# One attention stage of a sandwich block, its per-tile loop rewritten as seven steps that interleave two tiles

## The chip, the cores and the metric

The kernel runs on the 8 NeuronCores of one Trainium2 chip. Every core runs the same program on its own 2048 of the 16384 tokens, and the cores exchange nothing. The metric is the device time of the slowest core, in microseconds (us).

## The reference

```python
def attn(x, W_qkv, b_qkv, W_out, b_out):          # D_MODEL 1024, 16 heads of 64
    qkv = (x @ W_qkv + b_qkv).reshape(B, S, 16, 3 * 64)
    q, k, v = qkv[..., :64], qkv[..., 64:128], qkv[..., 128:]
    scores = einsum('bshd,bsgd->bshg', q, k) / 8   # over the heads of one token
    context = einsum('bshg,bsgd->bshd', softmax(scores), v)
    return context.reshape(B, S, 1024) @ W_out + b_out

def ffn(h, Wg, Wu, Wd):                            # 8 experts, FFN 4096, all summed
    for wg, wu, wd in zip(Wg, Wu, Wd):
        acc += (silu(h @ wg) * (h @ wu)) @ wd

x = x + layernorm(attn(layernorm(x)))
x = x + layernorm(ffn(layernorm(x)))
```

The attention is over the 16 heads of a single token, so no token looks at another. The scores are 16 x 16 for each token, and they are worked out on VectorE, with a token on each partition.

## The kernel before

The program has three stages. Stage A (lines 190 to 356) does the attention for 16 tiles of 128 tokens each, one tile after the other. Stage B (lines 402 to 489) is the FFN: for 64 groups of 512 hidden features (8 experts x 8 groups), and in each for 4 blocks of 512 tokens, TensorE makes 4 x 8 matmuls with Wg (L437), as many with Wu (L442) and 8 x 4 with Wd (L468). ScalarE applies silu, VectorE multiplies and adds into `acc` in SBUF. Stage C (lines 519 to 575) transposes `acc` back, normalises it, adds the residual and stores.

The buffers of stage B lie where those of stage A lay. So the first weight load of stage B (L409) waits for the last transpose, the last transposed copy and the last statistic of stage A.

Each engine runs its instructions in the order in which the Python code appends them to that engine's list (`steps`). The helper `op(engine, function, channel)` appends an instruction that raises a semaphore, and `channel.wt(engine, token)` appends a wait for it. A wait therefore stands in one engine's list and holds all that is behind it there.

For one tile, stage A before the change does, in this order:

1. Line 201: `ln_stats` on the residual `xf`: a sum (VectorE L141), a square (ScalarE L143), a second sum (VectorE L145), small VectorE operations, Ln and Exp (ScalarE L153, L155), and L157. Then L205 writes the normalised tile `ln1` in bf16.
2. Lines 208 to 213: eight TensorE transposes of `ln1` (L181) and one VectorE copy to `ln1T` (L184).
3. Lines 216 to 233: the QKV projection. Six output pieces of 512 columns, each a bias matmul (L223) and 8 matmuls (L227) into one of two PSUM buffers `ps_mm`. ScalarE evacuates each piece to `qkv` (L232).
4. Lines 236 to 307: the attention itself, almost all of it on VectorE: `vtc` (L237), four products of q and k (L248) that are folded by additions (L252) and a sum (L257), the softmax with one Exp on ScalarE (L270), four products with v (L290), and their foldings (L294, L302) into `ctxt`.
5. Lines 309 to 325: eight transposes of `ctxt`, the copy to `ctxT` (L184), and the output projection, two pieces of a bias matmul (L319) and 8 matmuls (L322) into `ps_att`.
6. Lines 327 to 337: `ln_stats` on `ps_att`, the normalisation to `tmpl` (L332) and the residual addition into `xf` (L336).
7. Lines 339 to 355: `ln_stats` on the new `xf`, `ln2tok` (L343), eight transposes, and the copy to `ln2T` (L184). After every fourth tile SyncE spills `xf` to HBM (L352) and reloads it for the tiles two blocks later.

The second set of statistics shares this helper, so L141, L143 and L145 each occur three times in a tile. `qkv` has one buffer. The evacuation of tile t into it waits for the end of tile t-1's attention (line 218).

Of the kernel before, what the change touches and what calls it, by code (L numbers as in the profile page):

```python
# [8 lines left out]
BF16 = mybir.dt.bfloat16  # L9
# [17 lines left out]
def build(mode='full', nt_lim=NT):  # L27
# [161 lines left out]
    ph = probsn  # L189
    for t_i in range(nt_lim):  # L190
        j, i = divmod(t_i, 4)
        jp = j % 2
        p2 = t_i % 2
        xt = xf[:, jp, i]

        if t_i == 0:
# [6 lines left out]
        if t_i >= 2:  # L203
            TB.wt('v', tok_ln1_tr[t_i - 2])
        w_ln1 = op('v', lambda v, xt=xt, p2=p2: v.tensor_scalar(  # L205
            ln1[:, p2], xt, stats[:, p2, 4:5], stats[:, p2, 5:6], ALU.mult, ALU.add), VE)

        VE.wt('t', w_ln1)
        if t_i == 0:
# [3 lines left out]
        trt, ev1 = transpose_batch(lambda k, p2=p2: ln1[:, p2, k * 128:(k + 1) * 128], ln1T[:, p2])  # L213
        tok_ln1_tr[t_i] = trt

        VE.wt('t', ev1)
        if t_i >= 1:
            VV.wt('s', tok_hm_done[t_i - 1])
        for n in range(6):
            b = n % 2  # L220
            if n_qg[0] - 2 in tok_qkv_evac:
                QE.wt('t', tok_qkv_evac[n_qg[0] - 2])
            op('t', lambda t, n=n, b=b: t.matmul(ps_mm[:, b], ones1[:],  # L223
                                                 bq_sb[:, n * 512:(n + 1) * 512], start=True, stop=False))
            mt = None
            for k in range(8):
                mt = op('t', lambda t, n=n, b=b, k=k, p2=p2: t.matmul(  # L227
                    ps_mm[:, b], ln1T[:, p2, k], wqkv_sb[:, k, n * 512:(n + 1) * 512],
                    start=False, stop=(k == 7)), MM if k == 7 else None)
            MM.wt('s', mt)  # L230
            tok_qkv_evac[n_qg[0]] = op(
                's', lambda s, n=n, b=b: s.activation(qkv[:, n * 512:(n + 1) * 512], ps_mm[:, b], AF.Copy), QE)  # L232
            n_qg[0] += 1
        tok_qkv_mm[t_i] = MM.v

        QE.wt('v', tok_qkv_evac[n_qg[0] - 1])
        op('v', lambda v: v.tensor_copy(  # L237
            vtc[:].rearrange("p (d g) -> p d g", g=16),
            bass.AP(qh, 128, [[H3, 128], [1, 64], [192, 16]])), VV)
        for grp in range(4):  # L240
# [3 lines left out]
            if gg - 2 in tok_prod:  # L244
                VV.wt('v', tok_prod[gg - 2])
            qap = bass.AP(qh, 192 * h0, [[H3, 128], [192, 4], [0, 16], [1, 64]])
            kap = bass.AP(qh, 64, [[H3, 128], [0, 4], [192, 16], [1, 64]])
            op('v', lambda v, sl=sl, qap=qap, kap=kap: v.tensor_tensor(  # L248
# [366 lines left out]
```

How the kernel before makes its waits and increments, by code:

```python
        def wt(self, k, tok=None):  # L70
            t_ = self.v if tok is None else tok
            em(k, lambda e, h=self.h, t=t_: e.wait_ge(h, t))
# [1 line left out]
    def op(k, fn, ch=None, n=1):  # L74
        if ch is not None:
            ch.v += n
            em(k, lambda e, fn=fn, h=ch.h, n=n: fn(e).then_inc(h, n))
            return ch.v
        em(k, fn)
        return None
```

## Time and profile before

| What | us |
|---|---|
| Runs shown (three) | 7185.4, 8108.4, 8331.37 |
| Median of the runs shown | 8108.4 |
| The profiled execution's own time | 7185.4 |
| Its span, slowest core (the others 7173.8 to 7182.2) | 7183.8 |
| TensorE busy in the span | 5686.8 (79%) |
| VectorE busy in the span | 3208.4 (45%) |
| ScalarE busy in the span | 781.6 (11%) |

The span is the time from the first to the last instruction of a core. The profiled execution is the fastest of the three shown. Busy time is the sum of the durations of an engine's instructions. Matmuls are pipelined and their ends are modelled, so a busy TensorE is not one at its peak. PE stands for TensorE, PEld for its weight loads, DVE for VectorE, ACT for ScalarE, POOL for GpSimd and SP for SyncE. L and a number is a line of the kernel.

### The profile page before, as it was taken

Reading aid. Unit: us, or ns where it says so; the run is one execution under the profiler, and the core shown is the slowest. Engines: PE = TensorE matmul, PEld = TensorE weight load, DVE = VectorE, ACT = ScalarE, POOL = GpSimd, SP = SyncE. Lnnn points to the kernel's source line nnn. Section 1 sums busy time; section 2 is a strip of 40 time slices with the busy share of each in tenths; the row PEclk is TensorE's granted clock in tenths of the full one; section 3 lists DMA queues with packets and bytes.
Section 4 is the critical chain, followed back from the end, with each engine's and each line's share of the span. In section 5 each row is a group of like instructions: output and inputs, shape, how many; then the busy total and the mean of one; then the engine's idle time right before and its main releaser. Section 6 shows DMA issues by size and latency. Waiting matters only on the chain.

```text
span 7183.8 us, 70830 instructions; the slowest of 8 cores (7173.8 to 7183.8 us)
## 1 busy us (share of the span) xinstructions
PE 5686.8 (79%) x25720; PEld 2568.3 (36%) x26240; DVE 3208.4 (45%) x4451; ACT 781.6 (11%) x1323; POOL 165.0 (2%) x202
## 2 busy tenths in 40 slices
PE   1222222224999999999999999999999999999992
PEld 0001000112444444444444444444444444444441
DVE  3665566554343343343343343343344343344346
ACT  0000000000111111111111111111111111111111
POOL 0000000000000000000000000000000000000000
PEclk7666555667999999999999999999999999999995
DMA  3000000002223222223222223222223222223212
GB/s 70 0 24 0 24 0 0 12 0 47 36 37 51 38 36 36 36 37 49 39 36 36 36 37 50 37 36 36 36 37 50 37 36 36 36 38 50 37 18 94
DMA packets 178221, 247.85 MB, mean 35 GB/s; under 512 B 3808, under 2 KB 134880, under 8 KB 177888
## 3 DMA queue, kind: packets, MB, share of 16 engines
q0 software_dynamic: 169056, 209.74, 18.5%
q1 hardware_dynamic: 8832, 33.56, 1.4%
q8 instruction: 223, 3.65, 0.2%
q14 instruction: 110, 0.90, 0.0%
HBM read 436.22 MB, written 16.78 MB: 63 GB/s over the span
## 4 chain that ended last, share of the span: by engine, by line
PE 79%; DVE 14%; issue 3%; ACT 2%; another core or an unknown queue 1%; DMA 0%; DVEq 0%; ACTq 0%; POOL 0%; POOLq 0%
PE ps_g L437 25%; PE ps_u L442 24%; PE ps_d L468 24%; PE ps_mm L227 3%; DVE prod L294 2%; DVE prod L252 2%; DVE prod L290 2%; DVE prod L248 2%; PE ps_att L322 1%; DVE stats L145 1%; DVE stats L141 1%; ACT scr L143 1%; PE ps_tr L181 1%; PE ps_mm L223 1%
## 5 line engine op out<-in xcount | busy, mean ns | idle before, releaser
L452 DVE TENSOR_TENSOR hbuf<-silb,ps_u 128x512 bf16<-128x512 bf16 x1024 | 704.9, 688 | 2885.6 <-PE ps_u L442 2768.8
L437 PE MATMUL ps_g<-ln2T,wg_b 128*128 128x512 bf16 x8030 | 1921.6, 379 | 43.5 <-DMA wd_b<-wd 35.0
L442 PE MATMUL ps_u<-ln2T,wu_b 128*128 128x512 bf16 x8028 | 1920.1, 379 | 8.6
L468 PE MATMUL ps_d<-hbuf,wd_b 128*128 128x512 bf16 x8027 | 1799.4, 379 | 8.7
L478 DVE TENSOR_TENSOR acc<-ps_d,acc 128x512 f32<-128x512 f32 x2016 | 1393.2, 692 | 330.7 <-PE ps_d L468 303.1
L437 PEld LDWEIGHTS ps_g<-ln2T,wg_b 128*128 128x128 bf16 x8192 | 801.8, 98 | 1002.5 <-issue 36.9
L442 PEld LDWEIGHTS ps_u<-ln2T,wu_b 128*128 128x128 bf16 x8192 | 801.7, 98 | 967.1 <-issue 1.1
L468 PEld LDWEIGHTS ps_d<-hbuf,wd_b 128*128 128x128 bf16 x8192 | 801.6, 98 | 966.5
L448 ACT ACTIVATE silb<-ps_g 128x512 bf16<-128x512 f32 x1024 | 611.4, 597 | 4675.4 <-PE ps_g L437 4489.2
L181 PE MATMUL ps_tr<-ident,ctxt 128*128 128x128 bf16 x128 | 16.2, 305 | 824.2 <-DVE ctxt L302 824.2
L181 PEld LDWEIGHTS ps_tr<-ident,ctxt 128*128 128x128 bf16 x128 | 12.4, 137 | 831.7 <-issue 831.7
L227 PE MATMUL ps_mm<-wqkv_sb,ln1T 128*128 128x512 bf16 x749 | 211.1, 429 | 2.1 <-issue 1.7
L409 POOL DMA_DIRECT2D wg_b<-wg x64 | 56.9, 890 | 6710.9 <-PE ps_d L468 5029.8
L181 PE MATMUL ps_tr<-ident,ln2tok 128*128 128x128 bf16 x128 | 16.2, 306 | 243.2 <-DVE ln2tok L343 243.2
L294 DVE TENSOR_TENSOR prod<-prod 128x2048 bf16<-128x2048 bf16 (+2 forms) x192 | 162.3, 845 | 20.7 <-DVE prod L294 0.9
L181 PE MATMUL ps_tr<-ident,ln 128*128 128x128 bf16 x128 | 16.2, 306 | 188.1 <-DVE ln L205 188.1
L252 DVE TENSOR_TENSOR prod<-prod 128x2048 bf16<-128x2048 bf16 (+2 forms) x192 | 149.9, 781 | 20.0
L290 DVE TENSOR_TENSOR prod<-probsn,vtc 128x4096 bf16<-128x4096 bf16 x64 | 146.3, 2286 | 3.7 <-DVE probsn L276 3.7
L248 DVE TENSOR_TENSOR prod<-qkv 128x4096 bf16<-128x4096 bf16 x64 | 146.1, 2282 | 0.0
L237 DVE COPY vtc<-qkv 128x1024 bf16<-128x1024 bf16 x16 | 16.4, 1025 | 261.5 <-ACT qkv L232 261.5
L227 PEld LDWEIGHTS ps_mm<-wqkv_sb,ln1T 128*128 128x128 bf16 x768 | 73.9, 107 | 115.5 <-issue 62.9
L539 PE MATMUL ps_c<-ident,acc_bf 128*128 128x128 bf16 x128 | 16.0, 307 | 114.7 <-DVE acctok L543 99.0
(71 smaller groups left out, 1016.5 us busy)
## 6 DMA issues: line engine op xcount, KB each, us to landing
wg_b<-wg POOLq DMA_DIRECT2D x64, 1024.0 KB, 10.9
wu_b<-wu POOLq DMA_DIRECT2D x64, 1024.0 KB, 15.2
wd_b<-wd POOLq DMA_DIRECT2D x64, 1024.0 KB, 19.3
xf<-x SPq DMA_DIRECT2D x4, 2048.0 KB, 13.7
xspill<-xf SPq DMA_DIRECT2D x4, 2048.0 KB, 8.1
xrel<-xspill SPq DMA_DIRECT2D x16, 512.0 KB, 4.3
out<-outb SPq DMA_DIRECT2D x16, 512.0 KB, 2.9
wqkv_sb<-wqkv POOLq DMA_DIRECT2D x1, 6144.0 KB, 53.8
```

The costliest lines, as they stand in the source:

```text
L181: tr_tok = op('t', lambda t, k=k, s_=s_: t.transpose(ps_tr[:, s_, k], src_fn(k), ident[:]), TB if k == 7 else None)
L227: mt = op('t', lambda t, n=n, b=b, k=k, p2=p2: t.matmul(ps_mm[:, b], ln1T[:, p2, k], wqkv_sb[:, k, n * 512:(n + 1) * 512], start=False, st ...
L248: op('v', lambda v, sl=sl, qap=qap, kap=kap: v.tensor_tensor(prod[:, sl].rearrange("p (h g d) -> p h g d", h=4, g=16), qap, kap, ALU.mult) ...
L252: op('v', lambda v, sl=sl, half=half: v.tensor_add(bass.AP(prod, sl * 4096, [[8192, 128], [1024, 4], [64, 16], [1, half]]), bass.AP(prod, ...
L290: op('v', lambda v, sl=sl, pap=pap, vap=vap: v.tensor_tensor(prod[:, sl].rearrange("p (h d g) -> p h d g", h=4, d=64), pap, vap, ALU.mult) ...
L294: op('v', lambda v, sl=sl, half=half: v.tensor_add(bass.AP(prod, sl * 4096, [[8192, 128], [1024, 4], [16, 64], [1, half]]), bass.AP(prod, ...
L437: gt = op('t', lambda t, par=par, kh=kh, kd=kd, bk=bk, toks=toks: t.matmul(ps_g[:, bk], wg_b[:, par, kd, kh * 128:(kh + 1) * 128], ln2T[:, ...
L442: ut = op('t', lambda t, par=par, kh=kh, kd=kd, bk=bk, toks=toks: t.matmul(ps_u[:, bk], wu_b[:, par, kd, kh * 128:(kh + 1) * 128], ln2T[:, ...
L448: silu_tok[c] = op('s', lambda s, bk=bk, c=c: s.activation(silb[:, c % 2], ps_g[:, bk], AF.Silu), SIL)
L452: mul_tok[c] = op('v', lambda v, kh=kh, bk=bk, c=c, q=q: v.tensor_tensor(hbuf[:, q % 2, kh], silb[:, c % 2], ps_u[:, bk], ALU.mult), MUL)
L468: dt_ = op('t', lambda t, par=par, m=m, mi=mi, kh=kh, q=q: t.matmul(ps_d[:, mi], wd_b[:, par, kh, m * 128:(m + 1) * 128], hbuf[:, q % 2, k ...
L478: tok = op('v', lambda v, m=m, mi=mi, toks=toks: v.tensor_add(acc[:, m, toks], ps_d[:, mi], acc[:, m, toks]), ACC)
```

## The change

The body of the loop over tiles is cut into seven functions, one for each step listed above: S1 (statistics and `ln1`), S2 (its transposes), S3 (QKV projection and evacuation), S4 (the attention on VectorE), S5 (transposes of `ctxt`, output projection), S6 (normalisation and residual addition), S7 (`ln2tok`, its transposes, the spill). A new loop calls them so that S6 and S7 of tile t-1 come after S3 of tile t, and S1 of tile t+1 comes before S4 of tile t. `qkv` gets a second buffer, and the evacuation of tile t waits for the attention of tile t-2. The operations and their shapes stay as they are. The reads of `qkv` on VectorE have a partition stride of two buffers (`2 * H3`), and an offset of `3072` elements for odd tiles.

```diff
-    qkv = Sa("qkv", [128, H3], BF16)
+    qkv = Sa("qkv", [128, 2, H3], BF16)
...
-    for t_i in range(nt_lim):
+    def S1(t_i):
...
+    def S3(t_i):
+        p2 = t_i % 2
+        VE.wt('t', tok_ln1T_ev[t_i])
+        if t_i >= 2:
+            VV.wt('s', tok_hm_done[t_i - 2])
...
             tok_qkv_evac[n_qg[0]] = op(
-                's', lambda s, n=n, b=b: s.activation(qkv[:, n * 512:(n + 1) * 512], ps_mm[:, b], AF.Copy), QE)
+                's', lambda s, n=n, b=b, p2=p2: s.activation(
+                    qkv[:, p2, n * 512:(n + 1) * 512], ps_mm[:, b], AF.Copy), QE)
...
+    def S4(t_i):
+        p2 = t_i % 2
+        QE.wt('v', tok_qkv_ev_last[t_i])
+        qb = 3072 * p2
...
-            qap = bass.AP(qh, 192 * h0, [[H3, 128], [192, 4], [0, 16], [1, 64]])
-            kap = bass.AP(qh, 64, [[H3, 128], [0, 4], [192, 16], [1, 64]])
+            qap = bass.AP(qh, qb + 192 * h0, [[2 * H3, 128], [192, 4], [0, 16], [1, 64]])
+            kap = bass.AP(qh, qb + 64, [[2 * H3, 128], [0, 4], [192, 16], [1, 64]])
...
+    def S6(t_i):
...
+        mt = tok_wout_mm[t_i]
         MM.wt('v', mt)
         MM.wt('s', mt)
...
+    S1(0)
+    for t_i in range(nt_lim):
+        S2(t_i)
+        S3(t_i)
+        if t_i >= 1:
+            S6(t_i - 1)
+            S7(t_i - 1)
+        if t_i + 1 < nt_lim:
+            S1(t_i + 1)
+        S4(t_i)
+        S5(t_i)
+    S6(nt_lim - 1)
+    S7(nt_lim - 1)
```

Each engine's list moves as follows. First TensorE, from the first output projection of stage A to the second tile's attention, in the kernel before (`ps_att` is the output projection, `ps_mm` the QKV projection, `ps_tr` a transpose):

```order
L322 MATMUL ps_att<-wout_sb,ctxT 128x512 x8
L319 MATMUL ps_att<-bo_sb,ones 128x512
L322 MATMUL ps_att<-wout_sb,ctxT 128x512 x8
L181 MATMUL ps_tr<-ident,ln2tok 128x128 x8
L181 MATMUL ps_tr<-ident,ln 128x128 x8
L223 MATMUL ps_mm<-bq_sb,ones 128x512
L227 MATMUL ps_mm<-wqkv_sb,ln1T 128x512 x8
```

The same place of the changed kernel, to the first piece of the QKV projection:

```order
L337 MATMUL ps_att<-wout_sb,ctxT 128x512 x8
L334 MATMUL ps_att<-bo_sb,ones 128x512
L337 MATMUL ps_att<-wout_sb,ctxT 128x512 x8
L184 MATMUL ps_tr<-ident,ln 128x128 x8
L231 MATMUL ps_mm<-bq_sb,ones 128x512
L235 MATMUL ps_mm<-wqkv_sb,ln1T 128x512 x8
```

And TensorE in the changed kernel from the last piece of that projection to the second tile's output projection:

```order
L231 MATMUL ps_mm<-bq_sb,ones 128x512
L235 MATMUL ps_mm<-wqkv_sb,ln1T 128x512 x8
L184 MATMUL ps_tr<-ident,ln2tok 128x128 x8
L184 MATMUL ps_tr<-ident,ctxt 128x128 x8
L334 MATMUL ps_att<-bo_sb,ones 128x512
```

The transposes of `ln2tok` moved from ahead of the next tile's QKV projection to behind it. The transposes of `ln1` and the QKV projection follow the output projection.

Next ScalarE, from the Exp of the first tile's softmax to the second tile's evacuations, in the kernel before (`scr` is the output of the squares, `qkv` that of the evacuations):

```order
L270 ACTIVATE probs<-sc 128x256
L143 ACTIVATE scr<-ps_att 128x1024
L153 ACTIVATE stats<-stats,consts 128x1
L155 ACTIVATE stats<-stats,consts 128x1
L143 ACTIVATE scr<-xf 128x1024
L153 ACTIVATE stats<-stats,consts 128x1
L155 ACTIVATE stats<-stats,consts 128x1
L143 ACTIVATE scr<-xf 128x1024
L153 ACTIVATE stats<-stats,consts 128x1
L155 ACTIVATE stats<-stats,consts 128x1
L232 ACTIVATE qkv<-ps_mm 128x512 x6
```

The same place of the changed kernel:

```order
L283 ACTIVATE probs<-sc 128x256
L240 ACTIVATE qkv<-ps_mm 128x512 x6
L143 ACTIVATE scr<-ps_att 128x1024
L153 ACTIVATE stats<-stats,consts 128x1
L155 ACTIVATE stats<-stats,consts 128x1
L143 ACTIVATE scr<-xf 128x1024
```

The six evacuations of tile t moved ahead of the square over `ps_att` that belongs to tile t-1. They stood behind all nine operations of the statistics before.

Last VectorE, at the end of the first tile's attention, in the kernel before:

```order
L302 TENSOR_TENSOR ctxt<-prod 128x256
L184 COPY ctxT<-ps_tr 128x1024
L141 TENSOR_REDUCE stats<-ps_att 128x1
L145 TENSOR_REDUCE stats<-scr 128x1
L146 TENSOR_SCALAR stats<-stats 128x1
```

The same place of the changed kernel:

```order
L315 TENSOR_TENSOR ctxt<-prod 128x256
L187 COPY ctxT<-ps_tr 128x1024
L187 COPY ln1T<-ps_tr 128x1024
L141 TENSOR_REDUCE stats<-ps_att 128x1
L145 TENSOR_REDUCE stats<-scr 128x1
L146 TENSOR_SCALAR stats<-stats 128x1
```

The copy of the next tile's `ln1T` moved up, between the copy of `ctxT` and the sum over `ps_att`.

## Rows read from the trace of the kernel before

**Rows 1.** The page: the span in 40 equal slices, in tenths.

```profile
PE   1222222224999999999999999999999999999992
DVE  3665566554343343343343343343344343344346
PEclk7666555667999999999999999999999999999995
```

**Rows 2.** Windows by stage of core 0; the columns are named in its header.

```profile
core 0: us, PE busy (x) PEld busy (x) DVE busy (x) ACT busy (x) POOL busy (x), PEclk, DMA share, GB/s
96.00:1609.73 1513.73, 365.50 (x1413) 141.30 (x1440) 917.06 (x1126) 133.52 (x240) 0.00 (x0) 0.60 0.02 7
1609.73:1719.81 110.08, 7.85 (x34) 3.49 (x35) 56.66 (x66) 3.67 (x7) 5.06 (x6) 0.54 0.32 54
1719.81:7150.00 5430.19, 5295.65 (x24205) 2416.74 (x24696) 2205.51 (x3208) 635.53 (x1058) 156.25 (x186) 0.99 0.24 40
```

**Rows 3.** Groups of instructions of 0 to 2200 us: line, operation, count, busy, mean, idle before.

```profile
L248 DVE TENSOR_TENSOR prod<-qkv 128x4096 bf16<-128x4096 bf16 x64 | 146.1, 2282 | 0.0
L141 DVE TENSOR_REDUCE stats<-ps_att 128x1 f32<-128x1024 f32 x16 | 19.6, 1225 | 108.1 <-PE ps_att L322 108.1
L237 DVE COPY vtc<-qkv 128x1024 bf16<-128x1024 bf16 x16 | 16.4, 1025 | 261.5 <-ACT qkv L232 261.5
```

**Rows 4.** One tile's instructions (`qkv`): duration ns min/median/max, first and last start us.

```profile
L237 DVE COPY vtc<-qkv x16: 1022/1024/1029, 96.0 to 1609.7; 128x1024 bf16<-128x1024 bf16 x16
```

**Rows 5.** Timeline from the second tile's attention to the third's: start, us, instruction, [idle before].

```profile
248.25 0.69 DVE L184 COPY ctxT<-ps_tr 128x1024 bf16<-128x1024 bf16 x1 [1.37 <-PE ps_tr L181]
...
255.32 1.23 DVE L141 TENSOR_REDUCE stats<-ps_att 128x1 f32<-128x1024 f32 x1 [6.38 <-PE ps_att L322]
256.63 1.02 ACT L143 ACTIVATE scr<-ps_att 128x1024 f32<-128x1024 f32 x1 [34.51 <-DVE stats L141]
...
269.16 0.81 DVE L343 TENSOR_SCALAR ln2tok<-xf,stats 128x1024 bf16<-128x1024 f32 x1
270.20 0.78 PEld L181 LDWEIGHTS ps_tr<-ident,ln2tok 128*128 128x128 bf16 x8 [15.49 <-issue]
...
278.62 1.01 PE L181 MATMUL ps_tr<-ident,ln 128*128 128x128 bf16 x8 [7.38 <-DVE ln L205]
...
280.72 0.58 PE L223 MATMUL ps_mm<-bq_sb,ones 1*128 1x512 bf16 x1 [1.09 <-DVE ln1T L184]
...
290.07 0.38 PE L223 MATMUL ps_mm<-bq_sb,ones 1*128 1x512 bf16 x1
...
292.22 0.38 PE L223 MATMUL ps_mm<-bq_sb,ones 1*128 1x512 bf16 x1
...
296.68 0.60 ACT L232 ACTIVATE qkv<-ps_mm 128x512 bf16<-128x512 f32 x1 [1.55 <-PE ps_mm L227]
297.38 1.03 DVE L237 COPY vtc<-qkv 128x1024 bf16<-128x1024 bf16 x1 [16.95 <-ACT qkv L232]
```

**Rows 6.** Windows of 1 us around the output projection of that tile; columns as in rows 2.

```profile
253.00:254.00 1.00, 1.00 (x6) 0.42 (x6) 0.00 (x0) 0.00 (x0) 0.00 (x0) 1.00 0.00 0
...
255.00:256.00 1.00, 0.21 (x1) 0.00 (x0) 0.68 (x1) 0.00 (x0) 0.00 (x0) 1.00 0.00 0
...
258.00:259.00 1.00, 0.00 (x0) 0.00 (x0) 1.00 (x2) 0.00 (x0) 0.00 (x0) 1.00 0.00 0
259.00:260.00 1.00, 0.00 (x0) 0.00 (x0) 0.42 (x4) 0.27 (x1) 0.00 (x0) 0.81 0.00 0
260.00:261.00 1.00, 0.00 (x0) 0.00 (x0) 0.38 (x2) 0.32 (x2) 0.00 (x0) 0.50 0.00 0
```

**Rows 7.** Windows of 1 us in the QKV projection that follows.

```profile
285.00:286.00 1.00, 1.00 (x3) 0.28 (x3) 0.00 (x0) 0.52 (x1) 0.00 (x0) 0.50 0.00 0
286.00:287.00 1.00, 1.00 (x4) 0.34 (x3) 0.00 (x0) 0.00 (x0) 0.00 (x0) 0.53 0.00 0
287.00:288.00 1.00, 1.00 (x6) 0.34 (x4) 0.00 (x0) 0.00 (x0) 0.00 (x0) 1.00 0.00 0
```

More of the change, by code:

```diff
@@ L169, in build @@
     tok_prod = {}
+    tok_ln1_w = {}
+    tok_ln1T_ev = {}
+    tok_qkv_ev_last = {}
     n_trb = [0]
@@ L204, in build, with S2 @@
             TB.wt('v', tok_ln1_tr[t_i - 2])
-        w_ln1 = op('v', lambda v, xt=xt, p2=p2: v.tensor_scalar(
+        tok_ln1_w[t_i] = op('v', lambda v, xt=xt, p2=p2: v.tensor_scalar(
             ln1[:, p2], xt, stats[:, p2, 4:5], stats[:, p2, 5:6], ALU.mult, ALU.add), VE)
-        VE.wt('t', w_ln1)
+    def S2(t_i):
+        p2 = t_i % 2
+        VE.wt('t', tok_ln1_w[t_i])
         if t_i == 0:
@@ L214, in build @@
         tok_ln1_tr[t_i] = trt
-        VE.wt('t', ev1)
-        if t_i >= 1:
-            VV.wt('s', tok_hm_done[t_i - 1])
+        tok_ln1T_ev[t_i] = ev1
+    def S3(t_i):
[3 more added lines that the diff above has]
+            VV.wt('s', tok_hm_done[t_i - 2])
         for n in range(6):
@@ L231, in build @@
             tok_qkv_evac[n_qg[0]] = op(
-                's', lambda s, n=n, b=b: s.activation(qkv[:, n * 512:(n + 1) * 512], ps_mm[:, b], AF.Copy), QE)
+                's', lambda s, n=n, b=b, p2=p2: s.activation(
+                    qkv[:, p2, n * 512:(n + 1) * 512], ps_mm[:, b], AF.Copy), QE)
             n_qg[0] += 1
         tok_qkv_mm[t_i] = MM.v
-        QE.wt('v', tok_qkv_evac[n_qg[0] - 1])
-        op('v', lambda v: v.tensor_copy(
+        tok_qkv_ev_last[t_i] = QE.v
+    def S4(t_i):
+        p2 = t_i % 2
+        QE.wt('v', tok_qkv_ev_last[t_i])
+        qb = 3072 * p2
+        op('v', lambda v, qb=qb: v.tensor_copy(
             vtc[:].rearrange("p (d g) -> p d g", g=16),
-            bass.AP(qh, 128, [[H3, 128], [1, 64], [192, 16]])), VV)
+            bass.AP(qh, qb + 128, [[2 * H3, 128], [1, 64], [192, 16]])), VV)
         for grp in range(4):
@@ L307, in build, with S5 @@
         tok_hm_done[t_i] = VV.v
+    def S5(t_i):
+        p2 = t_i % 2
         VV.wt('t', tok_hm_done[t_i])
@@ L325, in build @@
         tok_wout_mm[t_i] = mt
+    def S6(t_i):
+        j, i = divmod(t_i, 4)
+        jp = j % 2
+        p2 = t_i % 2
+        xt = xf[:, jp, i]
+        mt = tok_wout_mm[t_i]
         MM.wt('v', mt)
@@ L337, in build, with S7 @@
         VV.wt('v')
+    def S7(t_i):
+        j, i = divmod(t_i, 4)
+        jp = j % 2
+        p2 = t_i % 2
+        xt = xf[:, jp, i]
         ln_stats(lambda xt=xt: xt, p2)
```

## The prediction

> **What bounds the kernel now.** I read the slices of the page first [rows 1]. They show two regimes. For about nine slices VectorE is the busier engine, at 5 to 6 tenths, while TensorE is at 2 tenths. From the tenth slice on TensorE is at 9 tenths. The windows by stage [rows 2] say the same: between the first and the last `vtc` copy VectorE works for 917 of 1513.7 us and TensorE for 365.5, and in the FFN TensorE works for 5296 of 5430 us. The change touches the first regime alone, so at most a part of some 1600 us can move.
>
> The instructions of one tile give the period. The `vtc` copy occurs 16 times, from 96.0 to 1609.7 us [rows 4], which makes (1609.7 - 96.0)/15 = 100.9 us for each tile. VectorE is busy for 917/15 = 61 us of it. It has two large waits in a tile, both in the groups [rows 3]: 261.5 us in 16 times, or 16.34 us each, ahead of `vtc`, where it waits for the QKV projection and its evacuation, and 108.1/16 = 6.8 us ahead of the sum over `ps_att`, where it waits for the output projection. The rest is small: the waits within the statistics, and those for the transposes.
>
> The timeline [rows 5] shows a tile as one chain, in which each engine waits for the one before it. From the `ctxT` copy at 248.25 the output projection takes until the sum at 255.32. The square starts on ScalarE at 256.63, `ln2tok` at 269.16, the transposes of `ln1` at 278.62 and the QKV matmuls at 280.72. The last evacuation starts at 296.68 and `vtc` at 297.38. Nothing of tile t+1 runs beside tile t. The change offers that: QKV(t+1) next to the normalisation of tile t.
>
> **The change part by part.** The intended gain is the 16.34 us. While TensorE makes QKV(t), VectorE has S6 and S7 of tile t-1 to do, up to `ln2tok`: 269.16 + 0.81 - 255.32 = 14.7 us of chain [rows 5]. That work is not VectorE's alone, however. Its first step after the sum over `ps_att` is the square on ScalarE, and the new ScalarE list puts all six evacuations of QKV(t) ahead of that square. Each evacuation waits for its piece of the projection. The square therefore starts when QKV(t) is done, and VectorE, which needs the square for its second sum, stands still for the whole projection.
>
> What is left of the overlap is the sum over `ps_att` alone. From the start of the sum to that of the square are 256.63 - 255.32 = 1.31 us [rows 5]. In iterations 1 to 15 this sum runs beside QKV. In iteration 0 it is the first sum of S1(1), which I price alike. That gives 16 x 1.31 = 21 us off the path.
>
> The wait ahead of `vtc` goes to nothing, since S6, S7 and S1 stand between the evacuation and S4 now. It comes back as a wait ahead of the second sum (L145), of about 15 us in a tile. Behind that sum, S6, S7, S1, S4 and S5 follow each other as before, with the same links. S1(t+1) is no longer behind S7(t), but behind S7(t-1) in the same VectorE list, so it costs what it did. The transposes of `ln2tok` are behind QKV on TensorE, and by then QKV is over. The copy to `ln1T` now waits for the output projection and its transposes, as it would on the old chain, just in another place. All this is a sum of zero. The SyncE spills and reloads keep their order. The weight load that opens the FFN waits for the end of stage A as before, so the FFN shifts by what stage A gains and nothing else.
>
> The second term is TensorE's clock. The output projection starts at a granted clock of 0.5 (1.2 GHz), reaches 1.00 (2.4 GHz) in 253 to 254 us, keeps it after its last matmul in 255 to 256, and is at 0.81 and then 0.50 from 259 on [rows 6]. The QKV projection comes 25 us later in the kernel before and starts at 0.5 again: here it has 1.00 only from 287 on [rows 7], over 6 us after its first matmul. In the changed kernel it follows the output projection with only the transposes of `ln1` and one copy between them. By the rows that is from 278.62 to 280.72, or 2.1 us [rows 5], which is shorter than the 3 to 4 us for which the clock stayed at 1.00. So QKV should run at 2.4 GHz from its first matmul. A piece at that clock takes 292.22 - 290.07 = 2.15 us, and six take 12.9 us. What they take now: in the tile shown, 296.68 - 280.72 = 15.96 us of the 16.95 that VectorE waited [rows 5], so 0.99 us of the wait is something else, and the mean is 16.34 - 0.99 = 15.35 us. The gain is 15.35 - 12.9 = 2.45 us in each of 15 iterations, together 37 us. Its bounds are 0 (the clock falls in the gap) and 15 x (15.96 - 12.9) = 46 us.
>
> The eight transposes of `ln1` take 1.01 us at the low clock [rows 5]. At the full one they might take half, which is 0 to 15 x 0.5 = 8 us. I take 0, because the row nearest to them is at the low clock. The Trainium skill, "TensorE: Matmul & The Clock Gate", section "Part 4: PE-mode transpose", says that the full clock does not engage for transposes, since they do not count as TensorE activity in the same way. By that rule this term would be 0, and the transposes would do nothing to hold the clock through the gap; no row here shows transposes at the full clock.
>
> The wider `qkv` changes the partition stride of the reads in L237 and L248. The trace has no such read. The nearest row is L248 itself, 2282 ns x 64 = 146 us [rows 3], all on the path. A stride between partitions is the same work for each of them, so I take 0. The bounds are -5 and +5 us, from the spread of 7 ns around the mean of L237 [rows 4], with the doubling of L248 (+146 us) as the unlikely far end.
>
> The sum is 7185.4 - 21 - 37 = 7127 us. It is made against the profiled execution's own 7185.4 us, of which 7183.8 us are the span. The median of the three runs shown is 8108.4, 923 us higher, so the sum speaks for the level of the profiled execution. A tile's period should fall from 100.9 to about 97.2 us.
>
> **The rivals.** *The overlap works in full.* If ScalarE could do the square of tile t-1 between two evacuations, 16.3 us of wait would be under 14.7 us of statistics, and some 16.3 x 15 = 245 us would go: 7185 - 245 = 6940 us. For it speaks that VectorE and TensorE have no dependence on each other there. Against it stands the order of ScalarE's list, which has six evacuations in a row ahead of the square.
>
> *The clock falls in the gap.* The clock rose late in the tile shown, where the projection had itself kept TensorE busy for 6 us. If the short gap counts against it, QKV keeps its 15.35 us and only the first term is left: 7185 - 21 = 7164 us. Against it stands the time at 1.00 after the last matmul [rows 6].
>
> *The FFN gets a lower clock.* This is the case on the other side. Its place is the FFN, where the granted clock is 0.99 over 5430 us [rows 2], and its price is that of the runs shown at 8108 and 8331: 923 to 1146 us. With the gain of 58 taken off this gives about 8050 us. It would decide from a loss of 144 + 58 = 202 us on, which is a granted clock in the FFN of 0.99 x 5430/(5430 + 202) = 0.95. For it speaks that two of three runs are that long, which nothing in this trace accounts for. Against it stands that the FFN's instructions are the same in both kernels.
>
> The Trainium skill, "TensorE: Matmul & The Clock Gate", section "Seeing it yourself", says that a peak-current limit takes a die to 13/16 of the clock once three of its cores run dense matmuls. By that figure the FFN would take an estimated 5430 x 16/13 = 6683 us and the kernel about 8380. The trace disagrees for this execution, which held 0.99 [rows 2]; no row shown has the clock of the two longer runs.
>
> **How the numbers follow.** The forecast has 0.62, the clock that falls in the gap 0.18, the full overlap 0.07, the lower FFN clock 0.07, and 0.06 is for small mishaps that stay near the old time, the strided reads among them. A measurement of this kernel can tell about 2% from no change, which is 144 us. The forecast (0.8%), the case at 7164 and the mishaps are inside it: 0.86. Faster is the full overlap, 0.07. Slower is the FFN clock, 0.07. For the range I take both terms at their upper bounds, with the transposes (21 + 46 + 8 = 75 us), and 15 us for the spread between executions, of which the cores' 7173.8 to 7183.8 us give an idea: 7095 us. At the top it reaches over 7164 and the old time to 7205 us. The two cases at 6940 and 8050 us are left out.
>
> **What would show it.** In the new trace the idle time ahead of `vtc` should be near 0, and that ahead of L145 after the square over `ps_att` some 14 to 15 us in each of 15 iterations, with the square starting within 0.2 us of the last evacuation's end. The period between two `vtc` copies should be near 97 us. The first matmul of QKV should stand in a window with clock 1.00, and six pieces should follow 2.15 us apart. The FFN should still last 5430 us. The forecast is wrong if the square over `ps_att` starts before the last evacuation, if the QKV projection starts at 0.5, if L248 leaves 2282 ns, or if the FFN's clock leaves 0.99.

## The result and the profile after

| | Before | After |
|---|---|---|
| Shortest run, us | 7181.7 | 7109.1 |
| Median of all runs, us | 7430.1 (14 runs) | 7672.0 (12 runs) |
| Ratio at the same FFN clock | 1 | 0.9898 (95% interval 0.9882 to 0.9915) |

At the same clock in the FFN the change takes 1.0% off, 7184 to 7111 us or so, where I forecast 0.8% and 7127 us. The median of all runs is another matter. It went up by 242 us and lies far outside my range, because in most runs of either kernel some cores had a lower TensorE clock, above all in the FFN: 8 of the 14 runs before and 9 of the 12 after. The ratio compares only the other 6 and 3 runs.

The profiled execution after is one of the 9 (8236.7 us), so its span says nothing of the change. Its stage A does on core 7, where TensorE reached its full clock in that stage. First the slices of the page of the changed kernel, in tenths:

```profile
PE   1222222199999999999999999999999999999993
PEclk7555665588888888888888888888888888888885
```

Against rows 1 the clock in the FFN is at 8 tenths from its first slices on. The windows of core 7 for stage A and the FFN (columns: us, busy time of PE, PEld, DVE, ACT, POOL with counts, then PEclk, DMA share, GB/s) put a number to it:

```profile
98.20:1533.10 1434.90, 327.92 (x1440) 131.75 (x1440) 910.24 (x1119) 130.62 (x237) 0.00 (x0) 0.61 0.02 8
1643.50:8080.00 6436.50, 6434.37 (x24576) 2668.57 (x24574) 2120.59 (x3072) 614.92 (x1026) 156.31 (x186) 0.81 0.22 31
```

The FFN has 0.81 where [rows 2] had 0.99, and takes 6437 us where it took 5430. Stage A between the first and the last `vtc` copy takes 1434.9 us where it took 1513.7. The FFN's first matmul tells the same in one row, for the changed kernel (count, duration ns min/median/max, first and last start us):

```profile
L476 PE MATMUL ps_g<-ln2T,wg_b x8192: 379/437/631, 1643.0 to 8058.5; 128*128 128x512 bf16 x200
```

It starts at 1643.0 us. On core 0 it started at 1719.8 before [rows 2], 77 us later, but that is the latest core of the kernel before. Core 7 started at 1716.5 there and the mean of the eight cores is 1714.5, so stage A gained 71 to 74 us. This start doesn't depend on the FFN's clock, and I use it below as the measure of stage A.

It does depend on the clock in stage A, and there the cores of this execution differ. Cores 2, 3, 6 and 7 start the FFN at 1642.5 to 1643.8 us, cores 4 and 5 at 1670 to 1671, and cores 0 and 1 at 1690. On core 0 the QKV projection of one tile, the `vtc` copies and the FFN's first matmul show why:

```profile
1055.00:1067.00 12.00, 11.91 (x43) 4.09 (x42) 0.38 (x1) 2.39 (x4) 0.00 (x0) 0.81 0.00 0
L250 DVE COPY vtc<-qkv x16: 1016/1019/1021, 102.5 to 1581.2; 128x1024 bf16<-128x1024 bf16 x16
L476 PE MATMUL ps_g<-ln2T,wg_b x8030: 379/435/631, 1690.1 to 7845.3; 128*128 128x512 bf16 x196
```

The clock is at 0.81 in QKV, and the copies are (1581.2 - 102.5)/15 = 98.6 us apart, not 95.7 as on core 7. So the lower clock isn't confined to the FFN, and in stage A it cost this core 47 us. All starts of the FFN below are from cores that don't show this.

The groups of the changed kernel up to 1650 us show where the wait went:

```profile
L235 PE MATMUL ps_mm<-wqkv_sb,ln1T 128*128 128x512 bf16 x768 | 183.9, 383 | 0.0
L145 DVE TENSOR_REDUCE stats<-scr 128x1 f32<-128x1024 f32 x48 | 58.5, 1220 | 263.5 <-ACT scr L143 263.5
L141 DVE TENSOR_REDUCE stats<-ps_att 128x1 f32<-128x1024 f32 x16 | 19.4, 1215 | 6.8 <-PE ps_att L337 6.8
L250 DVE COPY vtc<-qkv 128x1024 bf16<-128x1024 bf16 x16 | 16.3, 1016 | 0.0
L187 DVE COPY ln1T<-ps_tr 128x1024 bf16<-128x1024 bf16 x16 | 11.1, 691 | 110.4 <-PE ps_tr L184 110.4
```

In the groups of the kernel before, L145 had this line:

```profile
L145 DVE TENSOR_REDUCE stats<-scr 128x1 f32<-128x1024 f32 x48 | 58.6, 1220 | 60.8 <-ACT scr L143 60.8
```

The 261.5 us ahead of `vtc` in [rows 3] are 0.0 now, and the wait ahead of L145, which waits for ScalarE, went from 60.8 to 263.5 us. The 108.1 us ahead of the sum over `ps_att` moved to the `ln1T` copy (110.4). So the wait has changed its place, and 202.7 of its 261.5 us came back.

The timeline of the changed kernel for one tile (start, us, instruction, [idle before]):

```profile
253.70 0.61 PE L184 MATMUL ps_tr<-ident,ln 128*128 128x128 bf16 x8
254.41 0.69 DVE L187 COPY ln1T<-ps_tr 128x1024 bf16<-128x1024 bf16 x1 [7.33 <-PE ps_tr L184]
255.02 1.21 DVE L141 TENSOR_REDUCE stats<-ps_att 128x1 f32<-128x1024 f32 x1
255.36 0.37 PE L231 MATMUL ps_mm<-bq_sb,ones 1*128 1x512 bf16 x1 [1.05 <-DVE ln1T L187]
...
257.49 0.38 PE L231 MATMUL ps_mm<-bq_sb,ones 1*128 1x512 bf16 x1
...
268.41 0.60 ACT L240 ACTIVATE qkv<-ps_mm 128x512 bf16<-128x512 f32 x1 [1.55 <-PE ps_mm L235]
268.90 1.02 ACT L143 ACTIVATE scr<-ps_att 128x1024 f32<-128x1024 f32 x1
270.02 1.22 DVE L145 TENSOR_REDUCE stats<-scr 128x1 f32<-128x1024 f32 x1 [13.79 <-ACT scr L143]
...
289.90 0.81 DVE L208 TENSOR_SCALAR ln<-xf,stats 128x1024 bf16<-128x1024 f32 x1 [0.18 <-DVE stats L157]
290.63 1.02 DVE L250 COPY vtc<-qkv 128x1024 bf16<-128x1024 bf16 x1
```

The sum over `ps_att` is done at 256.2, and its square starts at 268.90, directly behind the last evacuation. Between them VectorE does nothing for 13.8 us. QKV starts at 255.36 and its pieces are 2.13 us apart from the first on. It does so at the full clock, as the 1 us windows of the same tile show:

```profile
253.00:254.00 1.00, 1.00 (x10) 0.60 (x9) 0.00 (x0) 0.00 (x0) 0.00 (x0) 1.00 0.00 0
254.00:255.00 1.00, 0.31 (x6) 0.13 (x3) 0.59 (x1) 0.00 (x0) 0.00 (x0) 1.00 0.00 0
255.00:256.00 1.00, 0.64 (x3) 0.30 (x4) 1.00 (x2) 0.00 (x0) 0.00 (x0) 1.00 0.00 0
```

The means over tiles 1 to 14 of the starts in the two timelines (core 0 before, core 7 after) account for the whole period. Each row is a link of the chain in a tile, and each number the mean time from one start to the next.

| Link | Before, us | After, us |
|---|---|---|
| `vtc` to `ctxT` copy (the attention, transposes of `ctxt`) | 51.84 | 51.88 |
| `ctxT` copy to the end of the output projection's wait | 7.45 (to the sum over `ps_att`) | 7.92 (to the `ln1T` copy) |
| the sum over `ps_att` | 1.32 | beside QKV |
| `ln1T` copy to the end of the evacuations' wait | 17.02 (to `vtc`) | 14.49 (to the square) |
| square over `ps_att` to `ln2tok` | 12.71 | 12.61 |
| `ln2tok` to `ln2T` copy | 2.19 | 2.22 |
| `ln2T` copy to the write of `ln1` | 6.21 | 6.21 |
| write of `ln1` to what follows it | 2.21 (to the `ln1T` copy) | 0.73 (to `vtc`) |
| Sum | 100.95 | 96.06 |

That is 4.89 us in a tile, and 15 x 4.89 = 73 us. From the first to the last `vtc` copy the gain is 1513.7 - 1434.9 = 79 us, because S1 of the second tile now stands ahead of the first copy and no S1 ahead of the last.

### The profile page after: what moved, and what is told of

Read it like the earlier page. It is cut to its first block, busy times and chain, and to the rows that moved or that the text cites. A ratio compares the mean times of both kernels' runs of the same rounds, so it can differ in the third digit from the quotient of the medians.

```text
span 8235.1 us, 71349 instructions; the slowest of 8 cores (8018.4 to 8235.1 us)
## 1 busy us (share of the span) xinstructions
PE 6802.8 (83%) x26240; PEld 2822.3 (34%) x26240; DVE 3205.9 (39%) x4451; ACT 781.3 (9%) x1323; POOL 165.0 (2%) x202
## 4 chain that ended last, share of the span: by engine, by line
PE 82%; DVE 12%; issue 2%; ACT 1%; another core or an unknown queue 1%; DMA 0%; DVEq 0%; ACTq 0%; POOL 0%; POOLq 0%
PE ps_d L507 26%; PE ps_g L476 26%; PE ps_u L481 26%; PE ps_mm L235 2%; DVE prod L307 2%; DVE prod L265 2%; DVE prod L303 2%; DVE prod L261 2%; PE ps_att L337 1%; DVE stats L145 1%; ACT scr L143 1%; PE ps_tr L184 0%; DVE stats L141 0%; PE ps_mm L231 0%
## 5 line engine op out<-in xcount | busy, mean ns | idle before, releaser
L476 PE MATMUL ps_g<-ln2T,wg_b 128*128 128x512 bf16 x8192 | 2322.4, 435 | 34.4 <-DMA wd_b<-wd 34.4
L481 PE MATMUL ps_u<-ln2T,wu_b 128*128 128x512 bf16 x8192 | 2322.5, 436 | 0.0
L507 PE MATMUL ps_d<-hbuf,wd_b 128*128 128x512 bf16 x8192 | 2189.8, 436 | 0.0
L476 PEld LDWEIGHTS ps_g<-ln2T,wg_b 128*128 128x128 bf16 x8192 | 889.4, 109 | 1289.1 <-issue 1269.8
L507 PEld LDWEIGHTS ps_d<-hbuf,wd_b 128*128 128x128 bf16 x8192 | 889.8, 109 | 1255.8 <-issue 1242.2
L481 PEld LDWEIGHTS ps_u<-ln2T,wu_b 128*128 128x128 bf16 x8192 | 889.6, 109 | 1255.2 <-issue 1237.3
L235 PE MATMUL ps_mm<-wqkv_sb,ln1T 128*128 128x512 bf16 x768 | 183.9, 383 | 0.0
L145 DVE TENSOR_REDUCE stats<-scr 128x1 f32<-128x1024 f32 x48 | 58.5, 1220 | 263.5 <-ACT scr L143 263.5
L261 DVE TENSOR_TENSOR prod<-qkv 128x4096 bf16<-128x4096 bf16 x64 | 146.0, 2282 | 0.0
L240 ACT ACTIVATE qkv<-ps_mm 128x512 bf16<-128x512 f32 x96 | 57.4, 598 | 693.1 <-PE ps_mm L235 693.1
```

The source lines that it names most:

```text
L145: op('v', lambda v: v.reduce_sum(st_[:, 1:2], scr[:, par], axis=AX.X))
L235: mt = op('t', lambda t, n=n, b=b, k=k, p2=p2: t.matmul(ps_mm[:, b], ln1T[:, p2, k], wqkv_sb[:, k, n * 512:(n + 1) * 512], start=False, st ...
L261: op('v', lambda v, sl=sl, qap=qap, kap=kap: v.tensor_tensor(prod[:, sl].rearrange("p (h g d) -> p h g d", h=4, g=16), qap, kap, ALU.mult) ...
L476: gt = op('t', lambda t, par=par, kh=kh, kd=kd, bk=bk, toks=toks: t.matmul(ps_g[:, bk], wg_b[:, par, kd, kh * 128:(kh + 1) * 128], ln2T[:, ...
L481: ut = op('t', lambda t, par=par, kh=kh, kd=kd, bk=bk, toks=toks: t.matmul(ps_u[:, bk], wu_b[:, par, kd, kh * 128:(kh + 1) * 128], ln2T[:, ...
L507: dt_ = op('t', lambda t, par=par, m=m, mi=mi, kh=kh, q=q: t.matmul(ps_d[:, mi], wd_b[:, par, kh, m * 128:(m + 1) * 128], hbuf[:, q % 2, k ...
```

## The experiments

**e1, the old order with the new buffer.**

```diff
-    S1(0)
     for t_i in range(nt_lim):
-        S2(t_i)
-        S3(t_i)
-        if t_i >= 1:
-            S6(t_i - 1)
-            S7(t_i - 1)
-        if t_i + 1 < nt_lim:
-            S1(t_i + 1)
-        S4(t_i)
-        S5(t_i)
-    S6(nt_lim - 1)
-    S7(nt_lim - 1)
+        S1(t_i)
+        S2(t_i)
+        S3(t_i)
+        S4(t_i)
+        S5(t_i)
+        S6(t_i)
+        S7(t_i)
```

> The changed kernel with its steps called in the old order (S1 to S7 of one tile, then the next), so that only the two buffers of qkv and the wider partition stride of its reads are left of the change. Theory (the gain is the order of the steps, the buffer costs and gives nothing): the time of the kernel before, within 10 us at the same FFN clock, period between vtc copies 100.9 us, L261 at 2282 ns. Rival (part of the gain beyond the forecast, some 14 us, comes from the second buffer): 14 us faster, period 100.0 us.

The ratio to the kernel before was 1.0013 (0.9993 to 1.0033), and the shortest run 7183.8 us. The `vtc` copies of this kernel are (1610.7 - 97.0)/15 = 100.9 us apart:

```profile
L250 DVE COPY vtc<-qkv x16: 1022/1024/1026, 97.0 to 1610.7; 128x1024 bf16<-128x1024 bf16 x16
```

The period is that of the kernel before, and L261, the product of q and k with the wider stride, takes 2281 ns as against 2282. The buffer and the wider reads neither cost nor give anything that shows here. The gain is in the order.

**e2, the clock alone.** The kernel before, with TensorE kept busy from the output projection to the next QKV.

```diff
+    KW1, KW2 = 62, 30
+    def keep_warm(n):
+        QE.wt('t')
+        for _ in range(n):
+            op('t', lambda t: t.matmul(ps_mm[:, 0], ident[:], wqkv_sb[:, 0, 0:512],
+                                       start=True, stop=True))
...
         tok_wout_mm[t_i] = mt
+        if t_i + 1 < nt_lim:
+            keep_warm(KW1)
...
         tok_ln2_ev[t_i] = ev
+        if t_i + 1 < nt_lim:
+            keep_warm(KW2)
```

> The kernel before with 62 extra matmuls of 512 columns behind each output projection and 30 behind each set of ln2tok transposes, into a PSUM buffer that is overwritten, for tiles 0 to 14. Theory (the clock term by itself): QKV starts at a granted clock of 1.00, its six pieces stand 2.15 us apart, and both sets of transposes take about 0.6 us, so 15 x (2.45 + 2 x 0.4) = 49 us less than before at the same FFN clock, period 97.7 us. Rival (the faster QKV of the changed kernel has another cause than the clock, or the extra matmuls delay the transposes): no gain or slower, period 100.9 us or more.

The FFN started at 1688.3 us, 26 us ahead of the mean start before (1714.5). The period was (1579.3 - 94.5)/15 = 99.0 us, which is 29 us less in 15 tiles, and the only run without the lower clock took 7156.6 us, 25 us below the shortest beside it (7182.0). The sign was right and the size not much over half of the 49 us expected. The timeline in one tile, with the last extra matmuls (L193), the transposes and the first pieces of QKV, shows the reason:

```profile
267.60 6.64 PE L193 MATMUL ps_mm<-wqkv_sb,ident 128*128 128x512 bf16 x29
...
275.15 0.61 PE L181 MATMUL ps_tr<-ident,ln 128*128 128x128 bf16 x8 [0.92 <-DVE ln L213]
...
276.81 0.39 PE L231 MATMUL ps_mm<-bq_sb,ones 1*128 1x512 bf16 x1 [1.05 <-DVE ln1T L184]
277.14 3.52 PE L235 MATMUL ps_mm<-wqkv_sb,ln1T 128*128 128x512 bf16 x8
```

The transposes still ran at the full clock (0.61 us, not 1.01), but the first eight matmuls took 3.52 us. The clock had fallen some 2.8 us after the end of the last extra matmul (267.60 + 6.64 = 274.24), sooner than the 4 us in [rows 6], as the windows of this kernel say:

```profile
276.00:277.00 1.00, 0.19 (x1) 0.09 (x1) 0.56 (x1) 0.00 (x0) 0.00 (x0) 1.00 0.00 0
277.00:278.00 1.00, 1.00 (x4) 0.32 (x4) 0.00 (x0) 0.00 (x0) 0.00 (x0) 0.52 0.00 0
278.00:279.00 1.00, 1.00 (x4) 0.42 (x3) 0.00 (x0) 0.00 (x0) 0.00 (x0) 0.50 0.00 0
```

Over all tiles a QKV matmul took 408 ns here, as against 429 ns before and 383 ns in the changed kernel, so QKV got about half of what the full clock gives it. My rival of a clock that falls in the gap is therefore near. The gap from the end of the last matmul to QKV is 2.6 us here (274.24 to 276.81), and 1.5 us in the changed kernel (253.86 to 255.36). e8 tests a shorter one.

**e3 and e4, ScalarE's order.** Both leave every operation as it is and move entries of ScalarE's list. `Q6` and `Q7` are the squares of S6 and S7 with their waits, `L6` and `L7` their Ln and Exp, `E[n]` the evacuations, `w` the wait for the attention of tile t-2. The changed kernel's order is `w, E[0..5], Q6, L6, Q7, L7`. Each kernel has one of the two `for` lines.

```diff
+            del steps['s'][m0:]
+            for part in (Q6, L6, w, E[0], E[1], E[2], E[3], E[4], E[5], Q7, L7):    # in e3
+            for part in (Q6, w, E[0], L6, E[1], E[2], E[3], Q7, E[4], L7, E[5]):    # in e4
+                steps['s'].extend(part)
```

> The changed kernel with the three ScalarE operations of S6 (square over ps_att, Ln, Exp of tile t-1) put ahead of the six evacuations of tile t in ScalarE's list. Theory (ScalarE's order is what exposes QKV): S6 runs beside QKV, the first evacuation waits some 2.4 us and the projection ends some 1.2 us later, the square over xf starts about 7.0 us earlier in the tile: 15 x 7.0 = 105 us less than the changed kernel, period 88.7 us. Rival (something else holds VectorE there, such as the copies or TensorE): the time of the changed kernel, period 95.7 us.

> The changed kernel with the ScalarE operations of S6 and S7 put between the evacuations: square, evacuation 0, Ln and Exp, evacuations 1 to 3, square over xf, evacuation 4, Ln and Exp, evacuation 5. Theory: S6 and S7 up to ln2tok run wholly beside QKV, 12 to 12.6 us less in each of 15 tiles, 180 to 189 us less than the changed kernel, about 6925 us at the FFN clock of the profile before, period 83.4 us; the wait ahead of the second sum falls to about 1.3 us. Rival (TensorE becomes what is waited for, ahead of the ln2tok transposes): a gain of less than 150 us, and a wait of VectorE ahead of the ln2T copy. Rival (the order of ScalarE is not the cause): the time of the changed kernel.

e3: the FFN started at 1533.7 us, 109 us earlier than in the changed kernel, the period was (1425.1 - 100.7)/15 = 88.3 us, and the only run without the lower clock took 7003.5 us, 105.6 us below the changed kernel's shortest. Its timeline shows the late evacuation too:

```profile
254.09 1.07 ACT L240 ACTIVATE qkv<-ps_mm 128x512 bf16<-128x512 f32 x2
...
254.81 0.37 PE L231 MATMUL ps_mm<-bq_sb,ones 1*128 1x512 bf16 x1 [1.02 <-ACT qkv L240]
```

TensorE waits 1.02 us for a PSUM buffer. That was expected at 1.2 us.

e4: the FFN started at 1452.8 us, 190 us earlier than in the changed kernel, with a period of (1343.0 - 100.0)/15 = 82.9 us, and the only run without the lower clock took 6919.7 us, 189 us below 7109.1. The timeline of this kernel for one tile:

```profile
243.97 1.21 DVE L141 TENSOR_REDUCE stats<-ps_att 128x1 f32<-128x1024 f32 x1
...
245.28 1.02 ACT L143 ACTIVATE scr<-ps_att 128x1024 f32<-128x1024 f32 x1 [35.98 <-DVE stats L141]
246.40 1.22 DVE L145 TENSOR_REDUCE stats<-scr 128x1 f32<-128x1024 f32 x1 [1.22 <-ACT scr L143]
...
257.35 0.60 ACT L240 ACTIVATE qkv<-ps_mm 128x512 bf16<-128x512 f32 x1
...
257.79 0.81 DVE L369 TENSOR_SCALAR ln2tok<-xf,stats 128x1024 bf16<-128x1024 f32 x1
258.94 0.61 PE L184 MATMUL ps_tr<-ident,ln2tok 128*128 128x128 bf16 x8 [1.68 <-DVE ln2tok L369]
```

VectorE waits 1.22 us ahead of its second sum in place of 13.79, and `ln2tok` starts 0.4 us after the last evacuation does. The two chains end together. The transposes of `ln2tok` are near enough to QKV to run at the full clock now. This version is faster than both kernels.

**e5 to e7, the FFN's clock.** The FFN gets activations of zero, and every instruction stays.

```diff
-        ev = op('v', lambda v, s_=s_, dst=dst: v.tensor_copy(dst, ps_tr[:, s_]), VE)
+        if zero:    # given by the ln2T copy alone
+            ev = op('v', lambda v, s_=s_, dst=dst: v.tensor_scalar_mul(dst, ps_tr[:, s_], 0.0), VE)
+        else:
+            ev = op('v', lambda v, s_=s_, dst=dst: v.tensor_copy(dst, ps_tr[:, s_]), VE)
```

> The changed kernel with the ln2T copy multiplied by zero: the FFN's activations are all zero, so this leaves the FFN's values out, while every instruction of the FFN, its shapes and its weight loads stay. Theory (the runs at 7400 to 8300 us come from a limit on the current of dense matmuls with all eight cores, which depends on the data): the granted clock in the FFN is 0.99 in every run and core, and every run takes 7110 us within 20. Rival (the lower clock comes from outside the kernel's data, from the chip's state or from the mere rate of matmuls): about half of the runs are longer than 7350 us, as they are for the changed kernel (9 of 12) and for the one before.

> The kernel before with the ln2T copy multiplied by zero, so the FFN's values are left out and its instructions stay. Theory (with zero activations the FFN clock is 0.99 in every run, and the change is worth what stage A shows): every run near 7187 us, 73 to 77 us more than the 7113 us of the same edit on the changed kernel. Rival (the five equal runs of the zero FFN were luck or belong to the new order): runs above 7350 us among these.

> The kernel of e4_mixed (ScalarE's S6 and S7 operations between the evacuations) with the ln2T copy multiplied by zero, FFN values left out. Theory: every run at the same clock, 190 us less than the changed kernel with zero activations (7113), so 6923 us. Rival (part of the 190 us seen between FFN starts is given back later): more than 6940 us.

| Kernel with zero activations | Runs | Lowest to highest, us | Median, us |
|---|---|---|---|
| e6, before | 12 | 7181.6 to 7186.7 | 7182.5 |
| e5, changed | 5 | 7112.0 to 7113.6 | 7113.1 |
| e7, mixed | 5 | 6918.9 to 6949.8 | 6919.0 |

Of these 22 runs 21 lie within 5.2 us of the lowest of their kernel. Of the kernel before with its own data, 12 of 26 runs taken beside them stayed below 7290 us and the rest went up to 8331 us. So whether the FFN's clock falls depends on the data that its matmuls multiply, at the same instructions. The 22nd run is e7's 6949.8 us. In it cores 4 to 7 were some 20 to 32 us behind the others, at a mean clock of 0.907 as against 0.913. That is the size of a lower clock in stage A, where the data are the same as ever: in e4 cores 6 and 7 started the FFN 31 to 35 us late. No trace of that run was taken, so this is not shown.

The three kernels also stand apart cleanly now. From e6 to e5 are 7182.5 - 7113.1 = 69 us. e5 ran on another chip, and the kernel before took 7185.7 to 7186.7 us beside it, which makes the change worth 73 us. The mixed order is worth another 190 to 194 us. The ratio of e7 to the kernel before is 0.9642 (0.9621 to 0.9664).

**e8, the clock alone, with a shorter gap.** The kernel of e2 with more extra matmuls, and with the FFN on zeros as in e6.

```diff
-    KW1, KW2 = 62, 30
+    KW1, KW2 = 66, 33
```

> The kernel of e2_keep_warm with 66 and 33 extra matmuls in place of 62 and 30, and the ln2T copy multiplied by zero (FFN values left out). In e2 the clock fell in the 2.6 us between the last extra matmul and QKV in some tiles. Theory (that gap is what cost 18 of the 49 us): with 0.6 us less of it QKV has the full clock in nearly all tiles, 45 to 50 us less than the kernel before with zero activations. Rival (the transposes and the copy ahead of QKV let the clock fall whatever stands before them): still some 30 us.

The median was 7146.9 us, 35.6 us below e6. It is between the two numbers expected. Two groups of this kernel up to 1800 us give the reason:

```profile
L238 PE MATMUL ps_mm<-wqkv_sb,ln1T 128*128 128x512 bf16 x768 | 184.6, 384 | 0.0
L333 PE MATMUL ps_att<-wout_sb,ctxT 128*128 128x512 bf16 x256 | 94.7, 536 | 0.0
```

QKV is at 384 ns for a matmul, like the changed kernel's 383, so the clock held in all tiles. The gap between the last extra matmul and QKV is 1.9 us in this kernel (276.62 to 278.55 in one tile). But the output projection went from 502 ns in e6 to 536 ns, which takes back 16 x 0.034 = 0.5 us in a tile. It spends more of its matmuls at the low clock, and why it rises later there I did not settle. With QKV at 43 ns x 48 and its bias matmuls at 51 ns x 6 less (2.4 us), two sets of transposes (0.8 us) and the 0.5 us back, a tile should gain 2.6 us; the period went from 100.85 to (1569.8 - 96.3)/15 = 98.2 us.

**e9, a lighter FFN.** One matmul over a single partition ahead of each 16.

```diff
+            op('t', lambda t, bk=bk: t.matmul(ps_g[:, bk], ones1[:], bq_sb[:, 0:512],
+                                              start=True, stop=True))
...
+                if mi == 0:
+                    op('t', lambda t: t.matmul(ps_d[:, 0], ones1[:], bq_sb[:, 0:512],
+                                               start=True, stop=True))
```

> The changed kernel with one extra matmul over a single partition (1 x 512) ahead of each 16 matmuls of the FFN, 1536 in all, overwritten at once. Theory (the lower FFN clock is a limit on current, and a little less load avoids it): every run at a clock of 0.99 and at 7110 + 1536 x 0.215 = 7440 us. Rival (so small a reduction of load doesn't matter): more than half of the runs are longer than 7700 us, up to 8650 us.

The shortest of six runs took 7760 us, and the others up to 8970. Three of the six had the lower clock, so this edit does not avoid it. The price was wrong too: 7760 - 7110 = 650 us for 1536 matmuls is 0.42 us each, twice what I had put. The timeline of this kernel shows it around one extra matmul (L474):

```profile
3000.04 1.89 PE L483 MATMUL ps_u<-ln2T,wu_b 128*128 128x512 bf16 x8
3001.86 0.38 PE L474 MATMUL ps_g<-bq_sb,ones 1*128 1x512 bf16 x1
3002.18 1.90 PE L478 MATMUL ps_g<-ln2T,wg_b 128*128 128x512 bf16 x8
3003.92 1.89 PE L483 MATMUL ps_u<-ln2T,wu_b 128*128 128x512 bf16 x8
```

Eight matmuls without one beside them take 3003.92 - 3002.18 = 1.74 us. From 3000.04 to 3002.18 are 2.14 us, so the single one costs 0.40 us.

**e10 and e11, the share of runs with the lower clock.** The two kernels once more, unchanged, side by side.

> The changed kernel once more, next to e11 and the kernel before in the same rounds, for the share of runs with the FFN's clock at 0.81 in part of the FFN. Theory (the limit strikes either kernel alike, and the medians 7672 and 7430 differ by chance): the shortest runs at 7110 us, and about as large a share of runs below 7220 us as for the kernel before, near 4 in 10. Rival (the new order makes the lower clock likelier): no more than 2 in 10 of these runs are below 7220 us, and 4 in 10 or more of those of e11 are below 7290 us.

> The kernel before, handed in like the others, as the counterpart of e10. Theory: the shortest runs at 7184 us, a share of some 4 in 10 below 7290 us, like the 24 of 53 counted beside the other runs. Rival (kernels that are handed in have longer runs than the kernel before for a reason of the measurement, as the 4 of 11 of e1 and the 3 of 12 of the changed kernel would have it): clearly fewer than the kernel before has beside it.

The changed kernel had 1 of 8 runs near 7110 us, and a median of 7930. The kernel before had 3 of 12 near 7184 with a median of 7978 as e11, and 3 of 17 with a median of 8021 beside them. So side by side the two kernels were alike, and the median of the kernel before had itself moved by 590 us since the first comparison. Over all comparisons it is 4 of 20 for the changed kernel and 30 of 82 for the one before. That is no proof of equality; an effect of the order on this share is not excluded. But the gap between 7672 and 7430 needs none. The runs were made on several chips (chip 8 for e1 to e4, 12 for e5, 10 for e6 to e9, 7 for e10 and e11), and the kernel before had 9 of 17 runs near 7184 us on chip 10 and 6 of 29 on chip 7. Whether the chip decides this share was not tested.

## Why the prediction was wrong, and where it was right

**The step that failed** is the level. I wrote that "the sum speaks for the level of the profiled execution", gave the lower FFN clock a chance of 0.07, and left 8050 us out of the range, although two of the three runs shown were at 8108 and 8331 us. The runs showed that a run without the lower clock is the rarer one (34 of 102 for the two kernels together). The median after is 7672 us, outside 7095 to 7205, with the mechanism of the change itself as forecast. The evidence stood in the table: a range for the time of a run had to reach to 8250 us, whatever the change did. That the three short runs after lie at 7109 to 7111 us bears out the sum, not the range.

That rival gave its mechanism rightly in part. The place (the FFN) and the price (923 to 1146 us) are borne out in the main: the granted clock is 0.81 in the profile after, and groups of eight matmuls start 2.10 us apart there against 1.73 us. Stage A of some cores, with 47 us, comes on top. It is the 13/16 of the Trainium skill, "TensorE: Matmul & The Clock Gate", section "Seeing it yourself", and e5 to e7 bear out its remark that all-zero operands don't trip it, as far as the FFN goes. Where the Trainium skill says in that section that the limit comes within microseconds and holds while the load lasts, the runs differ, as below. "Slower" as a verdict on the change was wrong for this rival: it strikes both kernels.

**The wait that returns** was right. The wait ahead of `vtc` went to 0.0, and the wait ahead of L145 grew by (263.5 - 60.8)/15 = 13.5 us in a tile, where 14 to 15 were forecast. That ScalarE's list is the cause is shown by e3 and e4: moving entries of that list alone, with every operation kept, freed 109 and 190 us. With it falls the rival of a full overlap for this kernel. Its 6940 us are what e4 reached, at 6920, by another edit.

**The sum beside QKV** was right: 1.32 us a tile, 1.31 forecast.

**The clock term** was right: 17.02 to 14.49 us, or 2.53 us, where 2.45 were forecast. e8 shows that the clock alone brings a gain of this kind, and e2 that the rival (7164 us) was close: gaps of 1.5 us (the changed kernel) and 1.9 us (e8) held, and one of 2.6 us (e2) did not always hold. That the gap would be short enough was a reading of one tile [rows 6], in which the clock stayed up for 4 us; e2 had a tile in which it stayed up for 2.8 us, so the margin was smaller than I took it to be. The term also hangs on the run: on core 0 of the profile after, at 0.81 in stage A, the same link takes 17.02 us in the mean, and this gain is gone there.

**The terms put at zero** were mis-sized. The links that I called "a sum of zero" gave (7.45 + 2.21) - (7.92 + 0.73) = 1.0 us in a tile, or 15 us. The transposes of `ln1` are 0.4 us of it: 0.61 us at the full clock and not 1.01. I had taken 0 for them, and the Trainium skill, "TensorE: Matmul & The Clock Gate", section "Part 4: PE-mode transpose", says the full clock doesn't engage for transposes. The trace disagrees: they run faster when the clock is up. Whether they also help to hold it up, no run here shows. The other 0.6 us are, by the table, hand-overs between engines that went. TensorE no longer waits for the write of `ln1`, and `vtc` follows it on VectorE itself. With these 15 us the forecast of 58 becomes the 73 us of the table (72.6 between the shortest runs). The period forecast at 97.2 us is 96.1 us in the mean tile.

**The wider buffer** at 0 was right (e1, ratio 1.0013).

## What to carry to other kernels

When work of two tiles is interleaved, every engine's list has to be interleaved, not only that of the engine that waits. Here a good order for VectorE and TensorE was undone by six evacuations in a row on ScalarE, an engine that was busy 11% of the time, and moving a few of its entries was worth more than twice the whole change. And where the runs shown differ by 15%, settle what they differ in before a range is given; kernels whose FFN works on zeros agreed with themselves within 5 us in 21 of 22 runs, and show what a change elsewhere is worth.

## What the runs showed of the hardware

The granted clock of 0.81 is neither steady nor common to the cores, and it came to stage A too, with TensorE busy for about a quarter of the time (core 0 above). In e4 it came to core 4 in the midst of the FFN (the windows of core 4, columns as above):

```profile
2500.00:3200.00 700.00, 700.00 (x3245) 317.31 (x3244) 279.17 (x406) 80.59 (x135) 20.17 (x24) 1.00 0.26 37
3200.00:3500.00 300.00, 300.00 (x1321) 132.65 (x1319) 114.47 (x166) 32.84 (x55) 10.08 (x12) 0.95 0.30 43
3500.00:3700.00 200.00, 200.00 (x764) 82.82 (x762) 66.22 (x96) 18.51 (x31) 5.03 (x6) 0.81 0.23 32
```

In the same execution core 6 began the FFN at 0.81 and got its full clock back while it still worked:

```profile
3600.00:4000.00 400.00, 397.34 (x1495) 165.75 (x1524) 131.76 (x191) 37.94 (x64) 10.09 (x12) 0.81 0.21 32
4000.00:4400.00 400.00, 397.45 (x1564) 169.02 (x1594) 135.28 (x196) 40.26 (x68) 10.06 (x12) 0.85 0.21 32
4400.00:4800.00 400.00, 398.05 (x1818) 181.36 (x1854) 162.28 (x236) 45.37 (x76) 12.61 (x15) 1.00 0.27 40
```

It moves by pairs of cores. These are spans and clocks of the profiled execution of e10, in which cores 4 to 7 were left alone (7103.9 to 7108.1 us):

```profile
core 0: 7619.5 us, clock 0.836
core 1: 7622.8 us, clock 0.835
core 2: 7829.4 us, clock 0.814
core 3: 7829.7 us, clock 0.814
core 4: 7106.7 us, clock 0.902
```

The spans of cores 0 and 1 agree within 4 us, and so do those of 2 and 3, while the pairs differ by 207 us. The starts of the FFN in the profile after (1690 us on cores 0 and 1, 1670 us on 4 and 5) show the same pairs. All eight cores can also hold the full clock through the whole FFN, as in the profile before. What decides between the two in a given run stays open. Only the FFN's data and a small part of its load (e9) were varied to that end.
